# Cross-attention over 1500 keys: keys and values loaded in quarters of a chunk, one behind every slot, the mask's rows in thirds

## The chip, the core and the metric

The kernel runs on one core of one Trainium2 chip. The time is the device's, in microseconds, of one execution of the whole program: 32 batches, one launch. Durations inside it come from one profiled execution.

## What is computed

```python
# x (32, 56, 512), ctx (32, 1500, 512), all float32; 32 heads of 16
xn   = (x - mean(x)) * rsqrt(var(x) + 1e-5) * gamma + beta
Q    = split_heads(xn @ Wq.T)          # 32 heads
K, V = split_heads(ctx), split_heads(ctx)   # the context itself, no projection
s    = where(mask, einsum('bhsd,bhtd->bhst', Q, K) * 16**-0.5, -inf)
attn = einsum('bhst,bhtd->bhsd', softmax(s), V)
out  = x + attn.reshape(B, S, 512) @ Wout.T
```

The mask is of shape (32, 1500), one row per batch. Keys come in twice: once transposed by the host (`kt`, hidden dimension on the partitions), once as they are (`ctx`, used as values, keys on the partitions).

## The kernel before

**Tiling.** A batch has 1500 keys in 3 chunks of 500, and a chunk has 4 slots of 125 keys: 12 slots per batch, 384 in all. `kT` holds two batches of transposed keys, as [128 partitions, batch parity, chunk, 4 blocks of heads `g`, 4 slots `k`, 125 keys]: within a chunk the blocks come first, then the slots. `v_stage` has two stages of one chunk of values (125 partitions, 4 slots, 512 columns); GpSimd copies a chunk from there into `v` (L429), where each head's values stand beside ones, so that one matmul gives both the weighted sum and the denominator.

**A slot on TensorE** (its loop is the last block of the program): four score tiles for the maxima of a batch ahead (`score_tile`, L262, bf16, into two ring banks), four matmuls that spread the maxima (L295), 32 score matmuls (`score_blocks`, L303), 64 matmuls of the values of the slot before (`times_values`, L319), and in some slots a part of the output projection (L278). After the last of the values it raises `pv_done`, which so counts finished slots. The score tiles run a batch ahead: at the slots 10 and 11 of batch b they are those of batch b + 2, chunk 0; then chunk 0 goes on at slots 0 and 1 of batch b + 1, and so on.

**The other engines.** ScalarE makes the exponentials of a slot in two instructions (L385, L387), and at slot 0 it copies the sums of the batch before (L394). VectorE adds the mask's rows (`mask_tile`) to each score tile and takes its maximum in one instruction (L341), two instructions per tile with the readout; in slots 3 and 4 it also swaps (L370) and inverts (L377) the denominators of the batch before. GpSimd copies values (L429), spreads queries and maxima, and folds the sums (L438, L447, L450) and divides (L458).

**SyncE's queue** issues every DMA, in the order written out by hand at the end of its block. It waits for `pv_done` and then issues. In each batch b, at slot 0: the keys of batch b + 1, chunk 2 (1000 KB), the values of batch b, chunk 2 (1000 KB). At slot 4: keys of batch b + 2, chunk 0, values of batch b + 1, chunk 0, the mask's rows of batch b + 2 (112 partitions, 328 KB), and in even batches the store of a result and the load of a residual (224 KB each). At slot 8: keys of batch b + 2, chunk 1, values of batch b + 1, chunk 1. So 2 MB start in one go every four slots. `load_v` also waits for `v_ready`, GpSimd's copy out of the stage that is to be overwritten. Values of chunk c are copied by GpSimd (`spread_values`) in the order chunk 1 and 2 of batch b, then chunk 0 of batch b + 1; chunk 1's copy stands ahead of `fold_heads`, chunk 2's behind `divide_heads`.

The end of the program stores the last two results with the residual's load in between, when no keys or values move.

**Lines the prediction's steps touch:** L222 keys' load, L228 values' load, L231 mask's load, L237 residual's load, L241 result's store, and the lines above.

Of the kernel before, what the change touches and what calls it, by code (L numbers as in the profile page):

```python
# [18 lines left out]
BLOCKS, TILES_R, ROW = 4, 4, 32  # L19
# [69 lines left out]
def build(nc, x, kt, ctx, mask_lanes, mask_rows, wq_t, wout_t, gamma, beta, out):  # L89
    with ExitStack() as stack:  # L90
# [127 lines left out]
        out_rows = out.rearrange("(i b) s n -> i (b s) n", b=2)  # L218


        def load_k(sp, b, c):
            sp.dma_start(kT[:, b % 2, c].rearrange("p g k m -> p (g k m)"), kt[b, c]).then_inc(k_landed[b % 2][c], 16)  # L222

        def load_v(sp, b, c):
            n = CHUNKS * b + c
            src = ctx[b, KEYS * c:KEYS * (c + 1), :].rearrange("(m k) n -> m k n", k=CHUNK)
            wait_over(sp, v_ready, n - STAGES + 1)
            sp.dma_start(v_stage[0:LANES, n % STAGES], src).then_inc(v_landed[n % STAGES], 16)  # L228

        def load_mask(sp, b):  # L230
            sp.dma_start(mask_tile[0:PAIR_Q, b % 2, :], mask_add[b:b + 1].broadcast_to([PAIR_Q, CONTEXT])  # L231
                         ).then_inc(mask_tile_landed[b % 2], 16)

        def load_residual(sp, d):
# [15 lines left out]
        def score_tile(pe, unit):  # L250

            _, b, t = unit
            c, g, r = t // PAIRS, t % PAIRS // TILES_R, t % TILES_R
            if t == 0:
                pe.wait_ge(qdb_ready, b + 1)
            if t % PAIRS == 0:
                pe.wait_ge(k_landed[b % 2][c], 16 * (b // 2 + 1))
            bank = ring_bank(pe, unit)
            rows = slice(ROW * r, ROW * (r + 1))
            keys = kT[rows, b % 2, c, g].rearrange("p k m -> p (k m)").bitcast(BF16)  # L260
            keys = keys.rearrange("p (n h) -> p n h", h=2)[:, :, 1]
            nc.tensor.matmul(bank[0:PAIR_Q, 0:KEYS], qdb[rows, b % 2, g, :], keys,  # L262
                             start=True, stop=True).then_inc(ring_filled, 1)
# [19 lines left out]
        def begin_scores(pe, b, k):  # L283

            if k % CHUNK == 0:
                pe.wait_ge(k_landed[b % 2][k // CHUNK], 16 * (b // 2 + 1))
            if k == 0:
                pe.wait_ge(rows_spread, b + 1)
                pe.wait_ge(qd_ready, b + 1)
# [46 lines left out]
        def take_tile(dve, b, t, bank, sums):  # L336
            c, j = t // PAIRS, t % TILES_R * BLOCKS + t % PAIRS // TILES_R
            if t == 0:
                dve.wait_ge(mask_tile_landed[b % 2], 16 * (b // 2 + 1))
                wait_over(dve, neg_ready, b)  # L340
            nc.vector.tensor_tensor_reduce(  # L341
                out=sums, in0=bank[0:PAIR_Q, 0:KEYS],
# [79 lines left out]
        def spread_values(pool, b, c):  # L422

            n = CHUNKS * b + c
            pool.wait_ge(v_landed[n % STAGES], 16 * (n // STAGES + 1))
            wait_over(pool, pv_done, CHUNK * (n - CHUNKS + 1))
            halves = v[0:LANES, c].rearrange("p k i (h d) -> p (k i) h d", d=HEAD_DIM)[:, :, 0:3:2, :]
            staged = v_stage[0:LANES, n % STAGES].rearrange("p k (i h d) -> p (k i) h d", h=2, d=HEAD_DIM)
            nc.gpsimd.tensor_copy(halves, staged).then_inc(v_ready, 1)  # L429
# [34 lines left out]
        def _(sp):  # L464
# [9 lines left out]
            sp.dma_start(rows_u8[:, :], mask_rows).then_inc(mask_landed, 16)  # L474
            sp.dma_start(lanes_u8[0:LANES, :], mask_lanes).then_inc(mask_landed, 16)
            load_x(1)
            load_k(sp, 0, 0)
            for u in range(2, UNITS):
                load_x(u)
            load_k(sp, 0, 1)  # L480
            load_k(sp, 0, 2)
            sp.wait_ge(mask_added, 1)
            sp.dma_start(mask_add, rows_add[:, :]).then_inc(mask_stored, 16)
            load_k(sp, 1, 0)
            sp.wait_ge(mask_stored, 16)
            load_mask(sp, 0)
            load_mask(sp, 1)
            load_v(sp, 0, 0)
            sp.dma_start(woutT[:, :, :], wout_t.rearrange("(c p) n -> p c n", p=128)).then_inc(wout_landed, 16)
            load_k(sp, 1, 1)  # L490
            load_k(sp, 1, 2)
            sp.wait_ge(filled, FILLS)
            load_v(sp, 0, 1)
            load_v(sp, 0, 2)
            for b in range(BATCH):
                if b > 0:
                    if b < end:
                        sp.wait_ge(pv_done, SLOTS * b)
                        load_k(sp, b + 1, 2)
                    sp.wait_ge(pv_done, SLOTS * b)  # L500
                    load_v(sp, b, 2)
                if b < end:
                    sp.wait_ge(pv_done, SLOTS * b + CHUNK)
                    if b + 2 < BATCH:
                        load_k(sp, b + 2, 0)
                    load_v(sp, b + 1, 0)
                    if b + 2 < BATCH:
                        wait_taken(sp, ("tile", b, MAX_TILES - 1))
                        load_mask(sp, b + 2)
                if b % 2 == 0:  # L510
                    if b > 2:
                        store_result(sp, b // 2 - 2)
                    if b > 0:
                        load_residual(sp, b // 2 - 1)
                if b + 2 < BATCH:
                    sp.wait_ge(pv_done, SLOTS * b + 2 * CHUNK)
                    load_k(sp, b + 2, 1)
                if b < end:
                    sp.wait_ge(pv_done, SLOTS * b + 2 * CHUNK)
                    load_v(sp, b + 1, 1)  # L520
            store_result(sp, BATCH // 2 - 2)
            load_residual(sp, BATCH // 2 - 1)
            store_result(sp, BATCH // 2 - 1)
# [250 lines left out]
```

## Time and profile before

| | |
|---|---|
| median of 3 runs | 1591.01 us (1583.68 to 1594.36) |
| profiled execution, its own time | 1581.49 us |
| its span, first to last instruction | 1579.5 us |
| TensorE busy | 1390.2 us, 88% |
| VectorE busy | 1088.9 us, 69% |
| ScalarE busy | 769.3 us, 49% |
| GpSimd busy | 389.4 us, 25% |
| moved by DMA | 226.30 MB, mean 143 GB/s |
| DMA packets | 39249, of them 26882 of 2 to 8 KB |
| granted TensorE clock, mean | 0.934 |

The busy share of an engine says how full it is, not what it waits for; the views by wait, by queue and by stretch in the section below say that. The clock is the share of 2.4 GHz that was granted to TensorE.

### The profile page before, as it was taken

The page shows a single profiled execution, that of the slowest core. Times are in us where ns is not written, and L with a number is a line of the kernel's source. Part 1 is how long each engine was busy: PE and PEld are TensorE (multiplying, and loading weights), DVE is VectorE, ACT ScalarE, POOL GpSimd, SP SyncE. Part 2 cuts the span into 40 slices and gives each one's busy share as a digit, 9 for nine tenths or more (in the row PEclk, how much of TensorE's full clock was granted, in tenths as well). Part 3 has the DMA queues.
Part 4 walks back from the last instruction along what each step waited for, and adds up shares of the span by engine and source line. Part 5 has one row for each costly group of instructions (what it writes and reads, how often), then busy time and mean ns, then how long its engine had stood idle before and what let it go on. Part 6 is the DMA issues. An engine that isn't in the chain of part 4 may idle for free.

```text
span 1579.5 us, 88078 instructions
## 1 busy us (share of the span) xinstructions
PE 1390.2 (88%) x40736; PEld 1074.7 (68%) x40736; DVE 1088.9 (69%) x3452; ACT 769.3 (49%) x847; POOL 389.4 (25%) x371
## 2 busy tenths in 40 slices
PE   6999888899888988988888988989889888989986
PEld 4347767677676766766676776777677667767776
DVE  6557776777676767667777767777777676767741
ACT  2225454554554545454455545545454554544553
POOL 1012222332231133232133323222332231232221
PEclk8989998999999999899999999999999998998999
DMA  9214343443444444343434334344443443433420
GB/s 282 69 53 152 135 169 132 162 158 126 168 153 151 152 144 149 127 162 134 166 131 168 147 138 157 144 172 146 151 154 126 176 150 143 149 139 127 158 94 20
DMA packets 39249, 226.30 MB, mean 143 GB/s; under 512 B 4546, under 2 KB 4578, under 8 KB 26882
## 3 DMA queue, kind: packets, MB, share of 16 engines
q1 hardware_dynamic: 38882, 220.68, 38.4%
q8 instruction: 320, 5.24, 1.4%
q14 instruction: 47, 0.39, 0.1%
HBM read 216.90 MB, written 3.77 MB: 140 GB/s over the span
## 4 chain that ended last, share of the span: by engine, by line
PE 66%; DVE 23%; issue 9%; ACT 2%; DMA 0%; POOL 0%; SPq 0%; POOLq 0%; DVEq 0%; ACTq 0%
PE ps L319 21%; DVE masked L341 20%; PE ps L262 19%; PE ps L303 13%; PE ps L278 5%; PE ps L697 4%; PE ps L295 2%; DVE den_inv L377 2%; ACT probs L385 1%; PE ps L269 1%; DVE tile_max L341 1%; DMA v<-in_wq_t 0%; PE ps L688 0%; DVE den L370 0%; DVE probs L602 0%
## 5 line engine op out<-in xcount | busy, mean ns | idle before, releaser
L341 DVE CUSTOM_DVE_ANT_0 masked<-ps,mask_tile 112x500 bf16<-112x500 f32 x1536 | 974.2, 673 | 406.2 <-PE ps L262 391.0
L385 ACT ACTIVATE probs<-ps,mask_bias 125x1344 f32<-125x1344 f32 x384 | 530.3, 1381 | 711.9 <-PE ps L303 711.9
L262 PE MATMUL ps<-kT,qdb 32*112 32x500 bf16 x1536 | 498.3, 433 | 46.3 <-DVE tile_max L341 34.5
L303 PE MATMUL ps<-qd,kT 32*125 32x112 f32 x12288 | 498.6, 284 | 28.8 <-issue 28.6
L303 PEld LDWEIGHTS ps<-qd,kT 32*125 32x125 f32 x12288 | 494.9, 197 | 38.5 <-issue 34.1
L319 PE MATMUL ps<-probs,v 125*32 125x56 f32 x24576 | 429.3, 224 | 61.0 <-issue 59.1
L319 PEld LDWEIGHTS ps<-probs,v 125*32 125x32 f32 x24576 | 360.8, 117 | 159.9 <-issue 150.5
L262 PEld LDWEIGHTS ps<-kT,qdb 32*112 32x112 bf16 x1536 | 158.0, 128 | 203.4 <-DVE tile_max L341 150.0
L387 ACT ACTIVATE probs<-ps,mask_bias 125x448 f32<-125x448 f32 x384 | 240.4, 626 | 0.0
L295 PE MATMUL ps<-max_rows,ones_row 4*125 4x448 bf16 x1536 | 222.7, 400 | 11.6 <-issue 5.5
L429 POOL COPY v<-v_stage 125x2048 f32<-125x2048 f32 x96 | 181.5, 1891 | 75.5 <-DMA v_stage<-in_ctx 75.4
L418 POOL TENSOR_TENSOR max_rows<-rows,own_block 128x448 bf16<-128x448 f32 x32 | 29.8, 932 | 662.9 <-DVE rows L364 662.9
L341 DVE DVE_READ_ACCUMULATOR2_ANT tile_max<- 112x1 f32 x1536 | 126.6, 82 | 0.0
L458 POOL TENSOR_TENSOR attnT<-heads,den_inv 128x224 f32<-128x224 f32 x32 | 21.0, 656 | 366.9 <-DVE den_inv L377 366.9
L278 PE MATMUL ps<-woutT,attnT 128*112 128x128 f32 x512 | 76.3, 296 | 9.4 <-POOL attnT L458 5.1
L278 PEld LDWEIGHTS ps<-woutT,attnT 128*112 128x112 f32 x512 | 64.0, 189 | 25.5 <-DVE tile_max L341 12.9
L295 PEld LDWEIGHTS ps<-max_rows,ones_row 4*125 4x125 bf16 x1536 | 66.3, 135 | 18.6 <-issue 9.9
L697 PE MATMUL ps<-v 128*128 128x448 f32 (+2 forms) x160 | 66.9, 540 | 3.0 <-DMA v<-in_wq_t 2.2
L377 DVE RECIPROCAL den_inv<-den 128x56 f32<-128x56 f32 x128 | 62.9, 495 | 0.2
L358 DVE TENSOR_TENSOR result<-ps,x_res 112x128 f32<-112x128 f32 x64 | 18.6, 290 | 44.7 <-PE ps L278 41.5
L438 POOL TENSOR_TENSOR picked_den<-raw,own_head 128x448 f32<-128x448 f32 x32 | 29.8, 932 | 62.1 <-ACT raw L394 62.0
L662 ACT COPY qT<-ps 128x448 f32<-128x448 f32 (+2 forms) x20 | 9.1, 456 | 66.1 <-PE ps L697 65.9
(48 smaller groups left out, 293.5 us busy)
## 6 DMA issues: line engine op xcount, KB each, us to landing
kT<-in_kt SPq DMA_DIRECT2D x96, 1000.0 KB, 5.3
v_stage<-in_ctx SPq DMA_DIRECT2D x96, 1000.0 KB
mask_tile<-mask_add SPq DMA_DIRECT2D x32, 328.1 KB, 13.6
x_res<-in_x SPq DMA_DIRECT2D x16, 224.0 KB, 13.7
out<-result SPq DMA_DIRECT2D x16, 224.0 KB, 13.7
probs<-in_x SPq DMA_DIRECT2D x14, 224.0 KB, 9.8
v<-in_wq_t SPq DMA_DIRECT2D x1, 1024.0 KB, 6.7
woutT<-in_wout_t SPq DMA_DIRECT2D x1, 1024.0 KB, 20.3
```

The lines of the kernel that those rows point to most:

```text
L262: nc.tensor.matmul(bank[0:PAIR_Q, 0:KEYS], qdb[rows, b % 2, g, :], keys, start=True, stop=True).then_inc(ring_filled, 1)
L278: mm = nc.tensor.matmul(bank[0:PAIR_Q, 0:OUT_COLS], attnT[:, d % 2, g, :], woutT[:, g, OUT_COLS * part:OUT_COLS * (part + 1)], start=(g == ...
L295: nc.tensor.matmul(ps[0:LANES, score_bank(n, r), 0:BANK_Q], ones_row[rows, :], max_rows[rows, b % 2].rearrange("p g n -> p (g n)"), start= ...
L303: mm = nc.tensor.matmul(ps[0:LANES, score_bank(SLOTS * b + k, r), PAIR_Q * g:PAIR_Q * (g + 1)], kT[rows, b % 2, k // CHUNK, g, k % CHUNK, ...
L319: mm = nc.tensor.matmul(acc[ROW * r:ROW * (r + 1), i, :], v[0:LANES, c, k % CHUNK, TILES_R * g + r, HEAD_DIM * e:HEAD_DIM * e + ROW], prob ...
L341: nc.vector.tensor_tensor_reduce(out=sums, in0=bank[0:PAIR_Q, 0:KEYS], in1=mask_tile[0:PAIR_Q, b % 2, KEYS * c:KEYS * (c + 1)], scale=1.0, ...
L377: nc.vector.reciprocal(den_inv[:, g], den[:, g]).then_inc(den_inverted, 1)
L385: nc.scalar.activation(probs[0:LANES, k % PROBS, 0:HELD_ROWS], ps[0:LANES, 0:HELD_ROWS, 0:BANK_Q], ACT.Exp, bias=bias, scale=SCALE).then_i ...
L387: nc.scalar.activation(probs[0:LANES, k % PROBS, HELD_ROWS], ps[0:LANES, score_bank(n, HELD_ROWS), 0:BANK_Q], ACT.Exp, bias=bias, scale=SC ...
L418: nc.gpsimd.tensor_tensor(max_rows[:, b % 2], rows[:].unsqueeze(1).broadcast_to([128, BLOCKS, PAIR_Q]), own_block[:].unsqueeze(2).broadcas ...
L429: nc.gpsimd.tensor_copy(halves, staged).then_inc(v_ready, 1)
L697: mm = nc.tensor.matmul(bank, wqT[:, h, 128 * c:128 * (c + 1)], xT[u % 2][:, h, 0:w], start=(h == 0), stop=(h == BLOCKS - 1))
```

## The change

Every load of a chunk of keys or values becomes four loads of a quarter. A quarter of keys is one block `g` of heads (128 partitions, rows of 2000 bytes in place of 8000); a quarter of values is one slot `k` of the chunk (125 partitions, rows of 2048 bytes in place of 8192). A batch's mask rows come in three thirds, one per chunk (112 partitions, rows of 1000 bytes). The waits count all four or three pieces, so a consumer starts once the whole chunk, or the whole mask of a batch, has landed. In the loop SyncE waits for `pv_done` once per slot and issues one quarter of keys and one of values there; a third of the mask's rows goes behind slots 1, 4 and 7. Which chunk is loaded during which four slots is as before, so the first quarter starts where the whole chunk did, and the last one three slots later. The store and the residual stay at slot 4. The loads ahead of the loop keep their places, as runs of four or three.

```diff
-        def load_k(sp, b, c):
-            sp.dma_start(kT[:, b % 2, c].rearrange("p g k m -> p (g k m)"), kt[b, c]).then_inc(k_landed[b % 2][c], 16)
-
-        def load_v(sp, b, c):
+        def load_k(sp, b, c, g):
+            sp.dma_start(kT[:, b % 2, c, g].rearrange("p k m -> p (k m)"), kt[b, c, :, KEYS * g:KEYS * (g + 1)]
+                         ).then_inc(k_landed[b % 2][c], 16)
+
+        def wait_keys(pe, b, c):
+            pe.wait_ge(k_landed[b % 2][c], 16 * BLOCKS * (b // 2 + 1))
+
+        def load_v(sp, b, c, k):
             n = CHUNKS * b + c
             src = ctx[b, KEYS * c:KEYS * (c + 1), :].rearrange("(m k) n -> m k n", k=CHUNK)
-            wait_over(sp, v_ready, n - STAGES + 1)
-            sp.dma_start(v_stage[0:LANES, n % STAGES], src).then_inc(v_landed[n % STAGES], 16)
-
-        def load_mask(sp, b):
-            sp.dma_start(mask_tile[0:PAIR_Q, b % 2, :], mask_add[b:b + 1].broadcast_to([PAIR_Q, CONTEXT])
+            if k == 0:
+                wait_over(sp, v_ready, n - STAGES + 1)
+            sp.dma_start(v_stage[0:LANES, n % STAGES, k], src[:, k]).then_inc(v_landed[n % STAGES], 16)
+
+        def load_mask(sp, b, c):
+            keys = slice(KEYS * c, KEYS * (c + 1))
+            sp.dma_start(mask_tile[0:PAIR_Q, b % 2, keys], mask_add[b:b + 1, keys].broadcast_to([PAIR_Q, KEYS])
                          ).then_inc(mask_tile_landed[b % 2], 16)
...
             for b in range(BATCH):
-                if b > 0:
-                    if b < end:
-                        sp.wait_ge(pv_done, SLOTS * b)
-                        load_k(sp, b + 1, 2)
-                    sp.wait_ge(pv_done, SLOTS * b)
-                    load_v(sp, b, 2)
...
+                for k in range(SLOTS):
+                    step = k % CHUNK
+                    wait_over(sp, pv_done, SLOTS * b + k)
+                    if (b, k) >= (0, CHUNK):
+                        of, c = (b + 2, k // CHUNK - 1) if k >= CHUNK else (b + 1, CHUNKS - 1)
+                        if of < BATCH:
+                            load_k(sp, of, c, step)
+                        of, c = (b + 1, k // CHUNK - 1) if k >= CHUNK else (b, CHUNKS - 1)
+                        if of < BATCH:
+                            load_v(sp, of, c, step)
+                    if k in (1, 4, 7) and b + 2 < BATCH:
+                        if k == 1:
+                            wait_taken(sp, ("tile", b, MAX_TILES - 1))
+                        load_mask(sp, b + 2, k // 3)
+                    if k == CHUNK and b % 2 == 0 and b > 0:
+                        if b > 2:
+                            store_result(sp, b // 2 - 2)
                         load_residual(sp, b // 2 - 1)
```

## Rows read from the trace of the kernel before

**Rows 1.** The page and the cores: chain that ended last; span and mean clock.
```profile
PE 66%; DVE 23%; issue 9%; ACT 2%; DMA 0%; POOL 0%; SPq 0%; POOLq 0%; DVEq 0%; ACTq 0%
...
core 0: 1579.5 us, clock 0.934
```
**Rows 2.** Waits, whole span: who waited for what, us in total, times, longest.
```profile
PE ps L319 <- issue: 59.1, 46, 3.3
...
PE ps L303 <- issue: 28.6, 28, 3.0
```
**Rows 3.** Timeline of TensorE: start us, us, engine line op, shapes, count, idle before.
```profile
862.58 0.88 PE L319 MATMUL ps<-probs,v 125*32 125x56 f32 x51
866.07 0.39 PE L319 MATMUL ps<-probs,v 125*32 125x56 f32 x13 [2.62 <-issue]
```
**Rows 4.** Timeline of SyncE's queue, same columns, 856 to 858 us.
```profile
856.88 0.35 SPq L222 DMA_DIRECT2D kT<-in_kt  x1
857.27 0.33 SPq L228 DMA_DIRECT2D v_stage<-in_ctx  x1
857.65 0.31 SPq L231 DMA_DIRECT2D mask_tile<-mask_add  x1
```
**Rows 5.** DMA queues, 123.2 to 1486.2 us: kind: packets, MB, share of 16 engines.
```profile
q8 instruction: 296, 4.85, 1.5%
```
**Rows 6.** DMA queues, 857.3 to 863.2 us: the only two that moved anything.
```profile
q1 hardware_dynamic: 338, 1.62, 85.2%
q14 instruction: 1, 0.01, 0.4%
```
**Rows 7.** DMA queues, 863.2 to 866.1 us: the queue q8.
```profile
q8 instruction: 1, 0.02, 2.6%
```
**Rows 8.** Stretches: length, busy PE, PEld, DVE, ACT, POOL; clock, DMA share, GB/s.
```profile
859.00:861.00 2.00, 1.85 (x79) 1.54 (x83) 1.41 (x7) 1.77 (x2) 2.00 (x2) 1.00 0.97 362
864.00:869.00 5.00, 2.85 (x65) 1.94 (x69) 2.08 (x7) 0.98 (x1) 0.00 (x0) 0.88 0.34 136
867.78:874.61 6.83, 6.75 (x168) 5.40 (x169) 4.30 (x14) 3.24 (x4) 0.00 (x0) 0.50 0.19 76
874.60:912.10 37.50, 33.18 (x1074) 25.81 (x1066) 28.00 (x92) 20.11 (x23) 12.00 (x11) 1.00 0.44 160
1003.00:1048.00 45.00, 40.39 (x1309) 32.00 (x1309) 33.87 (x109) 23.35 (x25) 12.00 (x11) 1.00 0.44 160
1571.50:1572.00 0.50, 0.50 (x4) 0.50 (x4) 0.00 (x0) 0.00 (x0) 0.00 (x0) 0.50 0.99 283
```
**Rows 9.** Timeline of SyncE's queue: first and last load of keys in the loop.
```profile
123.20 0.35 SPq L222 DMA_DIRECT2D kT<-in_kt  x1
...
1486.24 0.35 SPq L222 DMA_DIRECT2D kT<-in_kt  x1
```
**Rows 10.** Timeline of ScalarE: slot 0 of two batches that follow each other.
```profile
980.22 1.38 ACT L385 ACTIVATE probs<-ps,mask_bias 125x1344 f32<-125x1344 f32 x1 [1.75 <-PE ps L303]
...
1022.89 1.38 ACT L385 ACTIVATE probs<-ps,mask_bias 125x1344 f32<-125x1344 f32 x1 [1.72 <-PE ps L303]
```
**Rows 11.** Timeline of TensorE, 980 to 1023 us: the instructions behind "issue".
```profile
1003.02 0.29 PE L319 MATMUL ps<-probs,v 125*32 125x56 f32 x4 [1.11 <-issue]
...
1020.75 0.59 PE L319 MATMUL ps<-probs,v 125*32 125x56 f32 x27 [0.27 <-issue]
```
**Rows 12.** The page, DMA issues: xcount, KB each, us from issue to landing.
```profile
kT<-in_kt SPq DMA_DIRECT2D x96, 1000.0 KB, 5.3
```
**Rows 13.** DMA queues, 1540 to 1563 us, the only one that moved anything.
```profile
q8 instruction: 7, 0.11, 2.2%
```
**Rows 14.** Timeline of GpSimd, 1021 to 1026 us.
```profile
1021.81 1.89 POOL L429 COPY v<-v_stage 125x2048 f32<-125x2048 f32 x1 [0.97 <-DMA v_stage<-in_ctx]
...
1025.37 0.93 POOL L438 TENSOR_TENSOR picked_den<-raw,own_head 128x448 f32<-128x448 f32 x1 [1.67 <-ACT raw L394]
```
**Rows 15.** Timeline of VectorE, 990 to 991 us.
```profile
990.42 0.41 DVE L370 STREAM_SHUFFLE den<-den_across 128x224 f32<-128x224 f32 x1
```

More of the change, by code:

```diff
@@ L256, in score_tile @@
             if t % PAIRS == 0:
-                pe.wait_ge(k_landed[b % 2][c], 16 * (b // 2 + 1))
+                wait_keys(pe, b, c)
             bank = ring_bank(pe, unit)
@@ L285, in begin_scores @@
             if k % CHUNK == 0:
-                pe.wait_ge(k_landed[b % 2][k // CHUNK], 16 * (b // 2 + 1))
+                wait_keys(pe, b, k // CHUNK)
             if k == 0:
@@ L338, in take_tile @@
             if t == 0:
-                dve.wait_ge(mask_tile_landed[b % 2], 16 * (b // 2 + 1))
+                dve.wait_ge(mask_tile_landed[b % 2], 16 * CHUNKS * (b // 2 + 1))
                 wait_over(dve, neg_ready, b)
@@ L424, in spread_values @@
             n = CHUNKS * b + c
-            pool.wait_ge(v_landed[n % STAGES], 16 * (n // STAGES + 1))
+            pool.wait_ge(v_landed[n % STAGES], 16 * CHUNK * (n // STAGES + 1))
             wait_over(pool, pv_done, CHUNK * (n - CHUNKS + 1))
@@ L476, in _ @@
             load_x(1)
-            load_k(sp, 0, 0)
+            for g in range(BLOCKS):
+                load_k(sp, 0, 0, g)
             for u in range(2, UNITS):
                 load_x(u)
-            load_k(sp, 0, 1)
-            load_k(sp, 0, 2)
+            for g in range(BLOCKS):
+                load_k(sp, 0, 1, g)
+            for g in range(BLOCKS):
+                load_k(sp, 0, 2, g)
             sp.wait_ge(mask_added, 1)
             sp.dma_start(mask_add, rows_add[:, :]).then_inc(mask_stored, 16)
-            load_k(sp, 1, 0)
+            for g in range(BLOCKS):
+                load_k(sp, 1, 0, g)
@@ L485, in _ @@
             sp.wait_ge(mask_stored, 16)
-            load_mask(sp, 0)
-            load_mask(sp, 1)
-            load_v(sp, 0, 0)
+            for c in range(CHUNKS):
+                load_mask(sp, 0, c)
+            for c in range(CHUNKS):
+                load_mask(sp, 1, c)
+            for k in range(CHUNK):
+                load_v(sp, 0, 0, k)
             sp.dma_start(woutT[:, :, :], wout_t.rearrange("(c p) n -> p c n", p=128)).then_inc(wout_landed, 16)
-            load_k(sp, 1, 1)
-            load_k(sp, 1, 2)
+            for g in range(BLOCKS):
+                load_k(sp, 1, 1, g)
@@ L492, in _ @@
+            for g in range(BLOCKS):
+                load_k(sp, 1, 2, g)
             sp.wait_ge(filled, FILLS)
-            load_v(sp, 0, 1)
-            load_v(sp, 0, 2)
+            for k in range(CHUNK):
+                load_v(sp, 0, 1, k)
+            for k in range(CHUNK):
+                load_v(sp, 0, 2, k)
             for b in range(BATCH):
-                if b > 0:
-                    if b < end:
-                        sp.wait_ge(pv_done, SLOTS * b)
-                        load_k(sp, b + 1, 2)
-                    sp.wait_ge(pv_done, SLOTS * b)
-                    load_v(sp, b, 2)
[L502 to L513, printed above, removed]
-                        load_residual(sp, b // 2 - 1)
[L515 to L520, printed above, removed]
```

## The prediction

> **What bounds the kernel now.** I read the page first, for the chain that ended last: it lies on TensorE for 66% of the span, on VectorE for 23%, and for 9% on "issue", which is time in which an engine waited for nothing that the profile shows; the granted clock averages 0.934 [rows 1]. The list of waits gives the matmuls of the values and of the scores 59.1 and 28.6 us behind "issue", in 46 and 28 stalls [rows 2]: few and long, 1.2 us each. No semaphore, bank or operand explains them, so I went to the timeline of one. TensorE stops inside the values of a slot, between the 51st and 52nd of 64 equal matmuls, for 2.62 us up to 866.07 [rows 3].
>
> The next view is the queue of SyncE. At 856.9 to 857.7 it began the keys, the values and the mask's rows of one step, 1000, 1000 and 328 KB [rows 4]. Then the DMA queues by packet. Queue q8, of kind "instruction", is the stream of TensorE's own instructions: between 123.2 and 1486.2 us it moved 296 packets of 16 KB [rows 5]. In the 5.9 us after the loads began it moved none [rows 6]. The next packet came in the 2.9 us after that [rows 7], and TensorE ran on at 866.07, inside the same stretch. So TensorE had used up its instructions and the next ones stood behind data. The table by stretch shows what they stood behind: from 859 to 861 us the DMA engines were busy to 97% [rows 8].
>
> The stall has a second price. Right behind it, from 867.78 to 874.61, the granted clock is 0.50 (1.2 GHz), where it was 1.00 (2.4 GHz) before [rows 8]. There TensorE issued 168 matmuls in 6.83 us, 24.6 per us; in the 37.5 us at full clock that follow it issued 1074, 28.6 per us [rows 8]. A stretch at half clock thus does 14% less. The mean clock of 0.934 [rows 1] means (1 - 0.934) x 2 x 1579.5 = 208 us at half clock, some 29 us of loss.
>
> **What the stalls cost in all.** First by batch, as that counts what the stalls drag along too. SyncE's first and last load of keys in the loop are at 123.20 and 1486.24 us [rows 9]; 90 of them make 89 steps of four slots, 356 slots of 12 to the batch, so a batch takes 1363.04 / 29.67 = 45.94 us. The batch whose first exponentials start at 980.22, the next batch's at 1022.89 [rows 10], took 42.67 us, with only two stalls in it, of 1.11 and 0.27 us [rows 11], and without a fall of the clock. Without them it is 42.67 - 1.11 - 0.27 = 41.29 us. The difference, 4.65 us, times 31.9 batches (383 slots from first to last) is 148 us. Second by parts: 59.1 + 28.6 of stalls [rows 2] and 29 of clock are 117 us, less than 148, since the slots behind a stall (scores, exponentials, VectorE's tiles) start late too. I take 148, as that stretch is the kernel itself at work with its bursts but nearly without stalls.
>
> **The change, part by part.** *Bytes* stay the same. *Keys*: one load of 1000 KB on four slots becomes four of 250 KB, one a slot. In before the load lands 5.3 us after its issue [rows 12]. A transfer of about the size of a quarter is seen at the end, where a result's store and a residual's load of 224 KB each follow each other: a half microsecond of that has the DMA engines at 99% [rows 8], at 283 GB/s; 448 KB at that rate are 1.6 us, 0.8 us for one and 0.9 us for a quarter. I take 1.0 us in which a fetch can be kept waiting, against 5.9 us behind keys and mask in the case above.
>
> *Values*: a quarter still goes in rows over 125 partitions. From 864 to 869 us, with the keys landed and values still moving, the DMA engines are busy to 34%, at 136 GB/s [rows 8]: the values use a third of them. Bounds: nothing, or 250 KB at 136 GB/s, 1.9 us a slot, if the fetch used those engines. I take nothing, since q8 delivered in that state [rows 7], as it did not while all were busy.
>
> *Mask*: 328 KB in one step become three of 109 KB in three slots, 0.4 us each at 283 GB/s, so that 1.0 us of keys is followed by 0.4 us of mask in three slots of twelve.
>
> *What is left of the stalls.* In 1540 to 1563 us, without data, q8 moved 7 packets in 23 us [rows 13], so instructions can come every 3.8 us or faster. A batch needs 296 / 29.67 = 10.0 packets, one in 4.1 us at 41.3 us a batch. The cover is 0.3 us. A slot of 3.4 us holds 1.0 us of keys, so a fetch meets them 29 times in 100 and is late by 0 to 1.0 us; what passes the cover is 0.29 x 0.7 x 0.7 / 2 = 0.07 us a fetch, 23 us over 319 fetches. The other bound is 0, since VectorE's tiles (23% of the chain [rows 1]) are the next limit in many slots and take in small holes. I take 6 us. Stalls so short should leave the clock alone: neither of the two in [rows 11] was followed by a fall, the clock being 1.00 from 1003 to 1048 us [rows 8].
>
> *Issues*: three more for keys, three more for values in every four slots, at 0.28 to 0.35 us [rows 4]: SyncE issues at most three in a slot, about 1.1 of 3.4 us, and nothing waits for it. At the start some 25 more issues of 0.4 us, 10 us together, are spread over the time in which TensorE works on its projections from inputs that have landed; that is their cover, and without it they would cost up to 10 us. I take 0.
>
> *Lateness*: the last quarter of each chunk is issued three slots later. The tightest is the second chunk of values. GpSimd copied it at 1021.81, and began the denominators at 1025.37 [rows 14]. Its last quarter would be issued one slot before the load at slot 0, about 1021.8. On a third of the engines 250 KB take about what 1000 KB of keys take on all, 5.3 us to landing: 1027.1, the copy ends at 1029.0, 3.6 us late, and the three steps up to their sum, at most 0.93 us each [rows 14], end at 1031.8. VectorE takes the denominators 10.2 us into a batch (990.42 [rows 15] less 980.22 [rows 10]), here at 1033.1. So it is hidden by 1.3 us; without that cover each us late costs up to 31 us over the kernel. Keys and mask of slot 7 are used at slot 10, two slots later.
>
> Sum: 1579.5 - 148 + 6 = 1437.5 us of span, plus 2.0 around it (1581.49 - 1579.5) gives 1439.5; stalls drag along some 26% more than themselves (148 to 117), so that the 1.38 us taken off the good batch should be 1.74, 0.36 x 31.9 = 11 us more, which gives 1428. I predict **1435 us**, between the two. The profiled execution lies 9.5 us under the median of the three runs, 1591.01, and within their range.
>
> **What the Trainium skill says.** Its page "Runtime: NRT & Kernel Launch", section "Instruction fetch mechanics", says that instructions come in blocks of 16 KiB, 256 instructions, with the next page fetched while the current one is executed; the trace agrees on the size (296 packets, 4.85 MB [rows 5]). It adds that the fetch is hidden behind the issuing of instructions; by that rule nothing is to be gained and the time would stay 1581.5. The stall in [rows 3, 6, 7] disagrees. Its page "DMA: Bandwidth & Descriptors", section "Queues, rings and completion order", says that each DMA engine takes turns between queues, and drains a whole packet of some 9 to 17 descriptors before it switches. By that, pieces of a quarter of the bytes make a turn shorter, which is this change's direction; that a fetch would get in between keys and mask is not what [rows 6] shows.
>
> **The rivals.** *Partial* (0.20): fetches still come late, each a little, because the cover is only 0.3 us and every slot now has a burst. If half of the 148 us stays, the time is 1581.5 - 74 = 1507. For it: 12 bursts a batch instead of 3. Against: each is a quarter as long.
> *No change* (0.06): the stall isn't set by the length of the bursts, or another wait takes its place, such as GpSimd's late values. Time 1575 to 1597.
> *Slower* (0.07): one mechanism, at the fetch. Bursts of keys come once a slot, and fetches once in 1.2 slots (10.0 to a batch); if nearly every fetch has to wait out a whole burst of 1.0 us, each loses 0.7 us past the cover, 319 x 0.7 = 223 us against 148 now, so 1581.5 + 75 = 1656 us. It decides from 0.46 us lost per fetch (148 / 319). Against: 29 in 100 is what chance gives.
> *Faster than forecast* (0.05): every slot as the quickest, no stall, under 1400 us.
> *The forecast* (0.62): 1400 to 1470.
>
> **How the numbers follow.** A measurement of this kernel can tell about 1% from no change. Forecast, faster case and the partial one lie all below -1%: 0.87. Within 1%: 0.06. Slower: 0.07. The range takes the forecast and most of the partial case, 1400 to 1525, some 0.8 in all.
>
> **What would show it.** Stalls behind "issue" on TensorE down from some 90 us to under 25; mean clock at 0.98 or above; q8 with a packet in every 5 us; batches of 40.5 to 42 us; loads of keys every 3.4 us. The forecast is wrong if q8 still pauses for 4 us or more, if the clock stays near 0.93, or if VectorE waits for the denominators.

## The result and the profile after

| | before | after |
|---|---|---|
| median | 1591.76 us (4 runs) | 1496.97 us (4 runs, 1490.18 to 1505.58) |
| ratio | 1 | 0.9415, 95% interval 0.9356 to 0.9475 |
| profiled execution, span | 1579.5 us | 1495.6 us |
| mean granted clock | 0.934 | 0.963 |
| stalls of the matmuls behind "issue", all lines | 98.0 us in 83 | 52.5 us in 73 |
| q1 (data), share of 16 engines' span | 38.4% | 47.7% |

The change is 5.9% faster, 95 us of the 156 that were forecast. The stalls and the clock both moved the forecast way and both stopped half-way. The rows below answer to [rows 1, 2, 12]. First the page of after: the chain by engine, and the keys' issues with count, size and landing.

```profile
PE 66%; DVE 26%; issue 6%; ACT 2%; DMA 0%; POOL 0%; SPq 0%; POOLq 0%; DVEq 0%; ACTq 0%
...
kT<-in_kt SPq DMA_DIRECT2D x384, 250.0 KB, 3.1
```

The waits of after, whole span:

```profile
PE ps L325 <- issue: 36.1, 44, 2.7
...
PE ps L309 <- issue: 13.4, 24, 2.3
```

"issue" went from 9 to 6% of the chain; the two waits fell from 87.7 to 49.5 us. A quarter of keys lands 3.1 us after its issue, a whole chunk took 5.3 [rows 12]: a quarter of the bytes needs 58% of the time.

The queue of SyncE, first and last load of keys in the loop, answers to [rows 9].

```profile
119.94 0.35 SPq L222 DMA_DIRECT2D kT<-in_kt  x1
...
1415.67 0.35 SPq L222 DMA_DIRECT2D kT<-in_kt  x1
```

Between them lie 359 slots: 1295.73 / 359 x 12 = 43.31 us a batch, where before took 45.94 and the forecast said 40.5 to 42.

Whose instructions q8 carries can be checked on all stalls. In before 72 of the 73 stalls of 0.3 us or more in the slots end 1.2 to 1.6 us after a packet of q8 has ended, in after 52 of 53 end 1.2 to 1.7 us after one. And from one such stall of before to the next TensorE starts 254 matmuls and weight loads, or a multiple of 254 to within 13, in 71 of 72 cases; 81,472 of them over the 320 packets of the whole run are 255 to a packet. So each stall stands at the end of a packet's worth of instructions and ends with the next packet.

Where the rest is. Sorted by slot (a slot counted from the start of its exponentials), the timeline of before gives 56 of its 98 us of stalls to slot 6, which comes behind the load of keys, values and mask at slot 4; the rest is spread. In after slot 6 still has 24 us, 22.7 of them in 14 stalls of even batches and only 1.7 in odd ones. Even batches are those that also store a result and load a residual at slot 4. One of them is batch 18. The timeline of SyncE's queue in after:

```profile
888.21 0.35 SPq L222 DMA_DIRECT2D kT<-in_kt  x1
888.60 0.33 SPq L233 DMA_DIRECT2D v_stage<-in_ctx  x1
888.97 0.50 SPq L237 DMA_DIRECT2D mask_tile<-mask_add  x1
889.52 0.42 SPq L247 DMA_DIRECT2D out<-result  x1
889.99 0.43 SPq L243 DMA_DIRECT2D x_res<-in_x  x1
```

The timeline of TensorE in after, the matmul behind the stall:

```profile
897.39 0.41 PE L325 MATMUL ps<-probs,v 125*32 125x56 f32 x7 [2.57 <-issue]
```

The stretches of after, columns as in [rows 8]:

```profile
890.50:892.50 2.00, 2.00 (x85) 1.69 (x89) 1.41 (x5) 1.59 (x2) 1.95 (x2) 1.00 0.85 86
892.50:894.50 2.00, 1.82 (x77) 1.29 (x76) 2.00 (x7) 1.12 (x1) 0.00 (x0) 1.00 0.93 209
897.40:904.00 6.60, 6.60 (x147) 5.79 (x150) 3.70 (x11) 1.91 (x2) 0.00 (x0) 0.52 0.37 113
```

The DMA queues of after from 889.9 to 895.3 us: packets, MB, share of 16 engines.

```profile
q1 hardware_dynamic: 627, 1.03, 93.0%
q8 instruction: 1, 0.02, 1.1%
```

Five loads and stores start within 1.8 us, and the DMA engines are busy to 85 and 93% for four microseconds, in the first two at only 86 GB/s. One packet of instructions began in these 5.4 us, at their end (894.82, 5.7 us after the one before it had ended), TensorE stood for 2.57 us, and the clock halved behind it. It is the picture of [rows 3 to 8] with less behind it.

Two ordinary slots of after, without mask or residual: the stretches that hold a quarter of keys (first and third) and those that do not.

```profile
701.50:703.00 1.50, 1.37 (x45) 0.79 (x43) 1.50 (x7) 0.80 (x1) 0.00 (x0) 1.00 0.75 209
703.00:704.90 1.90, 1.89 (x88) 1.65 (x80) 1.07 (x3) 1.58 (x3) 0.00 (x0) 1.00 0.35 125
704.90:706.50 1.60, 1.42 (x52) 0.89 (x52) 1.60 (x7) 0.94 (x1) 0.42 (x1) 1.00 0.67 190
706.50:708.00 1.50, 1.50 (x65) 1.21 (x57) 0.91 (x3) 0.97 (x2) 1.50 (x2) 1.00 0.34 131
```

The keys' burst takes 1.5 us, not the 1.0 of the forecast, and the values keep a third of the engines busy all the time between.

### The profile page after: what moved, and what is told of

Its sections match the earlier page's. It is cut to its first block, busy times and chain, and to the rows that moved or that the text cites. A ratio compares the mean times of both kernels' runs of the same rounds, so it can differ in the third digit from the quotient of the medians.

```text
span 1495.6 us, 88664 instructions
## 1 busy us (share of the span) xinstructions
PE 1352.0 (90%) x40736; PEld 1037.6 (69%) x40736; DVE 1088.4 (73%) x3452; ACT 769.7 (51%) x847; POOL 388.8 (26%) x371
## 3 DMA queue, kind: packets, MB, share of 16 engines
q1 hardware_dynamic: 125986, 220.71, 47.7%
## 4 chain that ended last, share of the span: by engine, by line
PE 66%; DVE 26%; issue 6%; ACT 2%; DMA 0%; POOL 0%; SPq 0%; POOLq 0%; DVEq 0%; ACTq 0%
DVE masked L347 22%; PE ps L325 22%; PE ps L268 21%; PE ps L309 12%; PE ps L284 5%; PE ps L707 4%; PE ps L301 2%; DVE den_inv L383 2%; ACT probs L391 1%; PE ps L275 1%; DVE tile_max L347 1%; DMA v<-in_wq_t 0%; DVE probs L612 0%; PE ps L698 0%; DVE den L376 0%
## 5 line engine op out<-in xcount | busy, mean ns | idle before, releaser
L309 PE MATMUL ps<-qd,kT 32*125 32x112 f32 x12288 | 478.7, 277 | 13.6 <-issue 13.4
L309 PEld LDWEIGHTS ps<-qd,kT 32*125 32x125 f32 x12288 | 475.1, 190 | 21.7 <-issue 18.0
L325 PE MATMUL ps<-probs,v 125*32 125x56 f32 x24576 | 410.4, 218 | 38.0 <-issue 36.1
L325 PEld LDWEIGHTS ps<-probs,v 125*32 125x32 f32 x24576 | 343.7, 113 | 132.7 <-issue 125.5
L301 PE MATMUL ps<-max_rows,ones_row 4*125 4x448 bf16 x1536 | 213.7, 391 | 7.9 <-ACT probs L391 5.5
L383 DVE RECIPROCAL den_inv<-den 128x56 f32<-128x56 f32 x128 | 63.1, 496 | 0.2
L707 PEld LDWEIGHTS ps<-v 128*128 128x128 f32 x160 | 27.5, 216 | 18.2 <-issue 12.5
```

Source lines behind the costliest of these rows:

```text
L301: nc.tensor.matmul(ps[0:LANES, score_bank(n, r), 0:BANK_Q], ones_row[rows, :], max_rows[rows, b % 2].rearrange("p g n -> p (g n)"), start= ...
L309: mm = nc.tensor.matmul(ps[0:LANES, score_bank(SLOTS * b + k, r), PAIR_Q * g:PAIR_Q * (g + 1)], kT[rows, b % 2, k // CHUNK, g, k % CHUNK, ...
L325: mm = nc.tensor.matmul(acc[ROW * r:ROW * (r + 1), i, :], v[0:LANES, c, k % CHUNK, TILES_R * g + r, HEAD_DIM * e:HEAD_DIM * e + ROW], prob ...
L383: nc.vector.reciprocal(den_inv[:, g], den[:, g]).then_inc(den_inverted, 1)
L707: mm = nc.tensor.matmul(bank, wqT[:, h, 128 * c:128 * (c + 1)], xT[u % 2][:, h, 0:w], start=(h == 0), stop=(h == BLOCKS - 1))
```

## The experiments

Two theories stood at the start. **A**: the packets of TensorE's instructions wait behind data on the DMA engine that carries them; keys, mask and residual pass over that engine, the values (over 5 engines) do not. **B**: any data in flight holds them. Each kernel was timed against the kernel before; ratios are to that.

| kernel | median us | ratio, 95% interval | stalls, matmuls, us (x) | clock |
|---|---|---|---|---|
| after | 1497.0 | 0.9415, 0.9356 to 0.9475 | 52.5 (73) | 0.963 |
| keys_only | 1562.0 | 0.9853, 0.9798 to 0.9908 | 87.0 (88) | 0.936 |
| values_only | 1575.9 | 0.9895, 0.9858 to 0.9932 | 92.9 (75) | 0.940 |
| mask_whole | 1509.5 | 0.9508, 0.9462 to 0.9554 | 63.1 (61) | 0.954 |
| halves | 1571.3 | 0.9904, 0.9872 to 0.9936 | 98.0 (107) | 0.955 |
| store_apart | 1477.4 | 0.9288, 0.9218 to 0.9357 | 44.2 (72) | 0.974 |
| eighths | 1517.2 | 0.9578, 0.9507 to 0.9650 | 59.2 (89) | 0.967 |
| before_eleven | 1656.6 | 1.0416, 1.0349 to 1.0482 | 133.2 (81) | 0.908 |
| one_row | 1424.9 | 0.8984, 0.8954 to 0.9014 | 10.9 (21) | 0.989 |
| values_real | 1437.7 | 0.9083, 0.9032 to 0.9134 | 18.4 (39) | 0.986 |

The stalls are the waits of TensorE's matmuls behind "issue" over the whole span of the profiled execution, all lines together. before_eleven is an edit of the kernel before, the others of after. one_row and values_real leave most of the input out, the others compute all of it.

### One part of the change alone

Keys in quarters, values and mask as before; and values in quarters, keys and mask as before. The edit to the changed kernel for the first (values and mask whole again):

```diff
-            sp.dma_start(v_stage[0:LANES, n % STAGES, k], src[:, k]).then_inc(v_landed[n % STAGES], 16)
+            if k % 4 == 0:
+                sp.dma_start(v_stage[0:LANES, n % STAGES, k:k + 4], src[:, k:k + 4]).then_inc(v_landed[n % STAGES], 16)
...
-                    if k in (1, 4, 7) and b + 2 < BATCH:
+                    if k == CHUNK and b + 2 < BATCH:
```

> Keys in quarters, one a slot; values whole (1000 KB) at slots 0, 4 and 8, mask whole at slot 4, so one part of the change alone. Theory A (TensorE's instruction packets wait behind data on the DMA engine that carries them, and only the keys, the mask and the residual use that engine): most of the gain is here, 1500 to 1530 us, with long stalls left only at the mask's step. Theory B (any data in flight slows the fetch, through memory or through the number of bytes in flight): values of 1000 KB in one go still stall it, about half the gain, 1540 to 1570 us.

And for the second (keys and mask whole again):

```diff
-            sp.dma_start(kT[:, b % 2, c, g].rearrange("p k m -> p (k m)"), kt[b, c, :, KEYS * g:KEYS * (g + 1)]
-                         ).then_inc(k_landed[b % 2][c], 16)
+            if g % 4 == 0:
+                sp.dma_start(kT[:, b % 2, c, g:g + 4].rearrange("p g k m -> p (g k m)"),
+                             kt[b, c, :, KEYS * g:KEYS * (g + 4)]).then_inc(k_landed[b % 2][c], 16)
```

> Values in quarters, one a slot; keys whole at slots 0, 4 and 8, mask whole at slot 4. Theory A: no gain, 1580 to 1600 us, stalls behind issue stay near 98 us and the clock near 0.93. Theory B: about half the gain, 1540 to 1570 us.

Measured: 1562.0 and 1575.9 us. For keys_only A asked for 1500 to 1530 us and is missed; 1562 lies in the range of B, but is a quarter of the change's gain and not half. values_only lies 4 us below A's range and far from B's; its stalls (92.9 us) and clock (0.940) are near those that A gave. Alone they give 1.5 and 1.1%, together, with the mask still whole (mask_whole, below), 4.9%. The parts need each other. The page of keys_only shows one reason, the landing of a quarter of keys, which took 3.1 us in after:

```profile
kT<-in_kt SPq DMA_DIRECT2D x384, 250.0 KB, 4.7
```

The packets of q8 show the rest. A chunk's loads begin at the slots 0, 4 and 8, 87 such steps in batches 1 to 29. Counted is how many packets start 2 to 4 us after TensorE has finished the slot before, when the load's data move. The matmuls and their order are the same in all these kernels, so one_row (below), with one row in each load, says what the program alone would give.

| kernel | keys | values | packets that start 2 to 4 us on |
|---|---|---|---|
| one_row | one row | one row | 39 |
| values_real | one row | quarters | 39 |
| after | quarters | quarters | 31 |
| halves | halves | halves | 21 |
| keys_only | quarters | whole | 19 |
| values_only | whole | quarters | 5 |
| before | whole | whole | 4 |

Whole keys keep the packets out, quarters of values keep none out, and whole values beside quarters of keys keep out more than quarters of both. So A holds where it says that keys hold the packets and that a load of values by itself doesn't. What it lacks is that whole values make the keys land later and hold longer. That they do so on the DMA engines that both use is argued from the landing times, not shown.

### One part of the change undone: the mask

```diff
-                    if k in (1, 4, 7) and b + 2 < BATCH:
-                        if k == 1:
-                            wait_taken(sp, ("tile", b, MAX_TILES - 1))
-                        load_mask(sp, b + 2, k // 3)
+                    if k == CHUNK and b + 2 < BATCH:
+                        wait_taken(sp, ("tile", b, MAX_TILES - 1))
+                        load_mask(sp, b + 2, 0)
```

> The changed kernel with the mask's rows whole again at slot 4 (328 KB): one part undone. Theory A: the stall in slot 6 grows by up to 0.8 us in every batch and is followed by half clock in odd batches too; 20 to 40 us more than the changed kernel, 1515 to 1535 us. Rival, that the thirds are worth nothing since each meets a page too: 1490 to 1505 us.

Measured: 1509.5 us, 12.5 more than after, under the 20 to 40 expected and above the rival's 1505, with intervals that overlap a little (0.9508 from 0.9462, 0.9415 to 0.9475). The direction is that of a burst at slot 4 that is longer; the size was overrated.

### Other sizes of a load

Halves: 500 KB of keys and of values behind every second slot. The edit to the changed kernel:

```diff
+            if g % 2 == 0:
+                sp.dma_start(kT[:, b % 2, c, g:g + 2].rearrange("p g k m -> p (g k m)"),
+                             kt[b, c, :, KEYS * g:KEYS * (g + 2)]).then_inc(k_landed[b % 2][c], 16)
...
+            if k % 2 == 0:
+                sp.dma_start(v_stage[0:LANES, n % STAGES, k:k + 2], src[:, k:k + 2]).then_inc(v_landed[n % STAGES], 16)
```

> The changed kernel with keys and values in halves of a chunk (500 KB), one of each behind every second slot; the mask's thirds, store and residual as there. A burst of keys lasts twice as long as a quarter, and there are half as many. Theory A with a cover of about 0.3 us: what counts is how far a fetch is kept waiting past its cover, and that grows faster than the burst; between the quarters and whole chunks, 1510 to 1540 us. Rival, that each burst costs the same whatever its length: half the loss of the quarters, 1455 to 1480 us.

Eighths: each quarter of keys in two loads, half a slot apart, with store and residual apart as in the next section.

```diff
+                        if of_k < BATCH:
+                            load_k(sp, of_k, c_k, step, (0,))
...
+                        if of_k < BATCH:
+                            sp.wait_ge(scored, SLOTS * b + k + 2)
+                            load_k(sp, of_k, c_k, step, (1,))
```

> The changed kernel with store and residual at slots 5 and 6, and each quarter of keys cut in two by slots of the chunk: one eighth (128 rows of 1000 bytes) ahead of the quarter of values, the other half a slot later, once the next slot's scores are made. To be compared with the kernel that only has store and residual apart, 1477 us. Theory A, bursts scale with the bytes: 1445 to 1465 us, clock 0.98 or more. Rival, a burst has a fixed part (first packets take several times as long as the later ones), so that halving the bytes leaves most of its length and doubles their number: 1475 to 1500 us.

Measured: halves 1571.3 us, 1.0% under before and worse than even A said: twice as many bursts as whole chunks, each landed 3.9 us behind its issue (5.3 whole), and as much stalled time in all (98.0 us against 98.0). Eighths 1517.2 us, against 1477.4 with quarters (store_apart): 40 us worse, beyond what its rival said. So neither longer nor shorter was better here. Why is not separated: both kernels also begin loads at other places of the program, eighths half-way through each slot. Shorter rows cost more engine time for the same bytes: 38.4% of 1579.5 us in before is 607, 47.7% of 1495.6 in after 713, 51.4% of 1515.8 in eighths 779. (Of before's 39249 packets 22304 are of 2 to 8 KB; the 26882 of its table are all those under 8 KB.) The data queue in the page of after (packets, MB, share):

```profile
q1 hardware_dynamic: 125986, 220.71, 47.7%
```

and in the page of eighths:

```profile
q1 hardware_dynamic: 181282, 220.73, 51.4%
```

### The step with five transfers

```diff
-                    if k == CHUNK and b % 2 == 0 and b > 0:
-                        if b > 2:
-                            store_result(sp, b // 2 - 2)
+                    if k == CHUNK + 1 and b % 2 == 0 and b > 2:
+                        store_result(sp, b // 2 - 2)
+                    if k == CHUNK + 2 and b % 2 == 0 and b > 0:
                         load_residual(sp, b // 2 - 1)
```

> The changed kernel with the result's store at slot 5 and the residual's load at slot 6 of even batches, in place of both at slot 4. In the changed kernel 11 of the stalls behind issue, 1.2 to 2.7 us each and some 21 us together, lie in slot 6 of even batches and are each followed by half clock. Theory A: they shrink below 1 us, the clock rises from 0.963 to 0.975 or more, and the time falls by 15 to 35 us to 1460 to 1482 us. Rival (the page boundary in slot 6 is late for another reason, such as the mask's third): no change, 1490 to 1505 us.

Measured: 1477.4 us, ratio 0.9288 (0.9218 to 0.9357): as expected, 20 us under after, though the intervals touch. Slot 6 of even batches went from 22.7 us of stalls in 14 to 3.2 in 6; the clock rose from 0.963 to 0.974. The other slots did not gain: 39.5 us in 63 stalls, where after had 28.1 in 56. The store and the residual may meet packets in their new slots; that is not shown. The waits of store_apart, whole span, are

```profile
PE ps L325 <- issue: 26.3, 46, 1.8
PE ps L309 <- issue: 15.1, 21, 1.9
```

and no stall above 1.9 us. It is the fastest kernel with the full computation here.

### What the traffic costs in all

The changed kernel with every load issued and waited for, but one partition's row in each from the third batch on; and the same with the values in full.

```diff
+            rows = 128 if b < 2 else 1
-            sp.dma_start(kT[:, b % 2, c, g].rearrange("p k m -> p (k m)"), kt[b, c, :, KEYS * g:KEYS * (g + 1)]
+            sp.dma_start(kT[0:rows, b % 2, c, g].rearrange("p k m -> p (k m)"), kt[b, c, 0:rows, KEYS * g:KEYS * (g + 1)]
```

> The changed kernel with the same loads issued and waited for, but from the third batch on each load of keys, values and mask brings one partition's row only (the rest of the tiles keeps older data, so most of the input is left out). It prices all that the traffic costs. Theory A: no stall behind issue but for those at the store and the residual of even batches, clock 0.98 or more, batches of 40.3 to 40.8 us, 1400 to 1430 us. Rival, that TensorE's instructions come late whatever the traffic: above 1450 us.

The second differs from the first in one line:

```diff
-            rows = LANES if n < 3 else 1
+            rows = LANES
```

> The changed kernel with all its loads issued, values in full quarters, but keys and mask of one row each from the third batch on (that part of the input is left out); residual and store in full. Against the run with one row of everything, 1425 us, it prices the values' quarters alone, which go over 5 engines. Theory A, as the prediction had it (values leave the instruction packets alone): 1420 to 1430 us. Theory C (the values' rows hold them too, which would explain that quarters of one kind alone gave 1.5% and 1.1% and both together 5%): 1440 to 1470 us.

Measured: 1424.9 and 1437.7 us. Without the traffic TensorE's instructions come in time: 10.9 us of stalls. The span and clock of one_row:

```profile
core 0: 1424.3 us, clock 0.989
```

The waits of one_row, whole span:

```profile
PE ps L328 <- issue: 7.5, 16, 1.4
PE ps L312 <- issue: 1.9, 2, 1.3
```

So data in flight costs the kernel before 1591.8 - 1424.9 = 167 us (160 by 1585.2, the median of its runs beside one_row) and the changed one 72 us. Of these 72 the values' quarters are 13 (between what A and C said, intervals 0.8954 to 0.9014 against 0.9032 to 0.9134), and keys, mask and the way they add up the other 59. Of the 72, 42 are stalls (52.5 - 10.9), and by the prediction's 14% some 11 are half clock; the remaining 19 are an estimate by difference. How the values' 13 us arise is open, as their quarters kept no packet out in the count above.

### Which DMA engine?

Four kernels loaded keys over fewer engines, as a load's partitions divide, to see which engine carries the instructions. How many engines a load uses can be read from its packets: in the third kernel the key packets in flight at once, in the middle of an undisturbed load, were 5, 6, 7, 9, 10, 11, 13, 14, 15 and 16 for 125, 102, 119, 81, 100, 110, 117, 126, 120 and 128 rows. The first is the kernel before with keys, mask, residual and store each in two parts, of 110 partitions and of the rest; the keys' part of the edit:

```diff
+            for p in (slice(0, 110), slice(110, 128)):
+                sp.dma_start(kT[p, b % 2, c].rearrange("p g k m -> p (g k m)"), kt[b, c, p]
+                             ).then_inc(k_landed[b % 2][c], 16)
```

> The kernel before, whole chunks in one go, but each load of keys cut by partitions into 110 and 18, and each load or store of mask, residual and result into 110 and 2: the same bytes at the same times, over fewer than 16 DMA engines (if the split follows the divisors of the partition count, 11 and 9 engines). Theory A with the instruction packets on an engine that these leave free: the stalls vanish without any quartering, clock 0.98 or more, 1400 to 1440 us. Theory A with the packets on one of the engines still used: no gain or a loss (bursts last 16/11 as long), 1580 to 1640 us. Theory B: no change, 1580 to 1600 us.

Measured: 1656.6 us, 4.2% slower than before and beyond the 1640 of its worst case, stalls 133.2 us. The 110 rows of the keys use 11 engines, each longer, and the packets are not free of them: 6 of the 87 steps counted above have one, where before has 4. It has the same bytes as before at the same slots, in bursts that are longer, but also in twice as many transfers.

The second gives each of a batch's three chunks of keys its own division:

```diff
+KEY_ROWS = [(102, 25, 1), (81, 27, 18, 2), (119, 7, 2)]
...
+            at = 0
+            for rows in KEY_ROWS[c]:
+                sp.dma_start(kT[at:at + rows, b % 2, c].rearrange("p g k m -> p (g k m)"), kt[b, c, at:at + rows]
+                             ).then_inc(k_landed[b % 2][c], 16)
+                at += rows
```

> The kernel before, with keys whole but cut by partitions so that each chunk's load uses another number of DMA engines: chunk 2 (slot 0) 119 + 7 + 2 rows, 7 engines; chunk 0 (slot 4) 102 + 25 + 1, 6 engines; chunk 1 (slot 8) 81 + 27 + 18 + 2, 9 engines. The keys on 11 engines still held the instruction packets back, the values on 5 do not. If an engine's place in the row is fixed and a load takes the first ones, the steps at which instruction packets start inside the keys' burst tell between which numbers the instruction packets' engine lies: free at all three: it is the tenth or eleventh; held at slot 8 alone: the eighth or ninth; held at slots 0 and 8: the seventh; held at all three: the sixth. If it is no fixed engine but the number of bytes in flight, the packets come late at all three alike.

Measured: 1680 us, one execution. The starts of q8's packets in the steps did not sort by 6, 7 and 9 engines; stalls were 98.0 us, as in before. The keys' packets of a chunk moved for 9.2 us in the median (3.6 in before) and the clock was 0.895; what of the loss is due to which was not separated. Inconclusive.

The third takes one_row and gives the keys back, whole chunks of as many rows as the list says, three batches (nine loads) for each entry:

```diff
+        KEY_ROWS = [125, 102, 119, 81, 100, 110, 117, 126, 120, 128]
...
+            if g % KEY_BLOCKS == 0:
+                rows = 128 if b < 2 else KEY_ROWS[(b - 2) // 3]
+                sp.dma_start(kT[0:rows, b % 2, c].rearrange("p g k m -> p (g k m)"), kt[b, c, 0:rows]
```

> From the third batch on only keys are loaded in bulk, whole chunks at slots 0, 4 and 8, and values and mask bring one row, so most of the input is left out. The number of partitions in the keys' load changes every three batches: 125, 102, 119, 81, 100, 110, 117, 126, 120, 128, which by their divisors are 5, 6, 7, 9, 10, 11, 13, 14, 15 and 16 DMA engines. Theory A with one fixed engine for TensorE's instructions: no stalls behind issue up to some number between 5 and 11, and from there on stalls of several us at nearly every load (bursts last 5 to 8 us on few engines). Rival, that the instruction packets go round the engines: stalls grow steadily with the number of engines. Rival, that it is the bytes in flight and no engine: stalls in all ten groups alike.

Measured: 1534.4 us, one execution. Stalled time per group of nine loads, in the order 125, 102, 119, 81, 100, 110, 117, 126, 120, 128 rows: 2.3, 4.1, 11.3, 3.0, 5.3, 9.4, 4.0, 5.7, 18.1, 4.4 us. The waits of TensorE in engines, first group (5 engines):

```profile
PE ps L332 <- issue: 1.9, 4, 0.9
PE ps L316 <- issue: 0.5, 1, 0.5
```

The same in its ninth group (15 engines):

```profile
PE ps L316 <- issue: 12.8, 5, 4.0
PE ps L275 <- issue: 3.7, 1, 3.7
PE ps L332 <- issue: 1.5, 4, 0.6
```

Five engines hold little, fifteen much, but there is no clean step and no steady growth. Nine loads are too few: where in a burst a packet falls depends on the program.

The fourth differs from the third in having two entries only, one for the even and one for the odd batches:

```diff
-                rows = 128 if b < 2 else KEY_ROWS[(b - 2) // 3]
+                rows = 128 if b < 2 else (102, 119)[b % 2]
```

> As the run with ten groups (only keys in bulk, whole chunks; most of the input left out), but with two sizes in turn: 102 partitions (6 engines) in even batches, 119 (7 engines) in odd ones. Both bring 17 rows of 8000 bytes to each engine used, bursts of the same length at the same places. Theory A with the instruction packets on the seventh engine alone: stalls of over 2 us only behind loads of 119 rows, and at least three times the stalled time there. With them on the sixth engine or below, or going round: both alike.

Measured: 1495.6 us, one execution; behind 45 loads of 102 rows 14.3 us in 21 stalls, one above 1.5 us; behind 45 of 119 rows 33.8 us in 27, seven above 1.5 us. A factor of 2.4 where A asked for 3, and one stall of 2.2 us where it allowed none. It leans to the seventh engine. Counted as above, of the 44 steps with 119 rows 4 have a packet 2 to 4 us on, where one_row has 22 at the same steps; but of the 43 with 102 rows 10 have one, against 17, so six engines seem to keep some out too, which the seventh alone can't explain. **Which engines carry the instructions stays open.**

## Why the prediction was right, and where it was not

- **What bounds the kernel: right.** Stalls behind "issue" are TensorE waiting for its instruction packets, held by data, with the clock as a second price. one_row shows it by taking the data away and leaving the work, the issues and the waits: stalls from 52.5 to 10.9 us, clock 0.989. The 72 of 73 stalls that end 1.2 to 1.6 us behind a packet of q8 show that it is this queue, and the count of packets (39 of 87 steps without keys, 4 with whole keys) that data hold it.
- **What the stalls cost, 148 us: nearly right.** Before less one_row is 160 to 167 us. The one good batch that the estimate rested on had 1.38 us of stalls in it and slots behind them that were late too; the 11 us added for that were in the right direction.
- **A quarter of keys, 1.0 us: too small.** Its burst is 1.5 us at 67 to 75% of the engines. The rate was taken from a half microsecond inside two transfers side by side (283 GB/s [rows 8]), where the start of one is covered by the other. Engine time for the same bytes grew from 607 to 713 us.
- **Values, nothing: the reason right, the size wrong.** Quarters of values alone keep no packet out (39 of 87 steps, as with none), as the reading of [rows 7] had it, yet values_real gives 13 us. And the values' size matters through the keys, which landed after 4.7 us beside whole values and after 3.1 beside quarters.
- **What is left of the stalls, 6 us: the step that failed.** It measured 72 us (1497.0 - 1424.9), with an upper bound of 23 in the working. Three things were wrong in it: 1.0 for 1.5 us; values at nothing; and chance as the rule for how packets meet bursts. A batch has 10.0 packets (296 / 29.67), nearly a whole number, so a packet's place in the program moves little from batch to batch: slot 6 was hit in 30 of 32 batches in before. If it falls behind the fullest step, it does so again and again. The step with store and residual had been left where it was and costed at nothing; store_apart prices it at about 20 us. Of the other 46 us (72 - 6 - 20) values_real gives the values 13; how the rest splits is not shown. The cover of 0.3 us was not too high: in one_row packets start as little as 3.3 us apart, under the 3.8 that were taken.
- **The clock stays up after short stalls: right for most.** But 11 stalls of slot 6 in even batches were 1.2 to 2.7 us, and 10 of them had a stretch of half clock of 3.4 or 6.8 us that began within them or up to 2 us behind. Seven more such stretches stood behind stalls of 0.6 to 1.1 us, where the prediction expected none. Mean clock 0.963, not 0.98.
- **Mask: direction right.** mask_whole costs 12.5 us more.
- **Lateness of the last values, hidden: right.** Batch 15 of after, whose slot 0 starts at 747.32, answers to [rows 14, 15]. The timeline of GpSimd:

```profile
751.50 1.89 POOL L435 COPY v<-v_stage 125x2048 f32<-125x2048 f32 x1 [5.71 <-DMA v_stage<-in_ctx]
...
755.14 0.66 POOL L453 TENSOR_TENSOR den_across<-picked_den 128x224 f32<-128x224 f32 x1
  ```

  The timeline of VectorE:

  ```profile
757.73 0.41 DVE L376 STREAM_SHUFFLE den<-den_across 128x224 f32<-128x224 f32 x1
```

  The sum of the denominators is there at 755.80, 1.9 us before it is taken; 1.3 had been worked out. In the whole run VectorE waits for it twice, 21.8 us, both behind 1438 us at the end, and before does so as well (twice, 20.5 us).
- **Issues and start, nothing: right.** The loop's first load of keys is at 119.94, earlier than before's 123.20.
- **Which case came.** The time is that of the rival called partial: 52.5 of 98.0 us of stalls are left, "each a little, because the cover is only 0.3 us and every slot now has a burst". It was given 1507 us and 0.20; the forecast's own 1400 to 1470 missed. Of the signs that it named for being wrong one came: q8 still paused for 5.7 us before the stall at 897.39. The batches of 43.31 us and the clock of 0.963 lie outside what it asked for as well. That the range of 1400 to 1525 holds 1497 is owed to the partial case, not to the sum.
- **The two rules of the Trainium skill.** That the fetch is hidden ("Runtime: NRT & Kernel Launch", "Instruction fetch mechanics") holds in one_row, at 11 us of stalls, and not beside loads. That an engine changes queues only after a packet of several descriptors ("DMA: Bandwidth & Descriptors", "Queues, rings and completion order") agrees in its direction: beside quarters 31 of 87 steps had a packet, beside whole loads 4. No run here shows the turns themselves.

## What to carry to other kernels

Where TensorE stalls for 1 to 3 us behind "issue" in the middle of equal matmuls, look at the queue of kind "instruction" and at what data transfers began in the 8 us before; then price it with a copy of the kernel whose loads bring one row. Cut such transfers to what the instruction stream can bear, all of them, since parts alone gave 1.5 and 1.1% and together 5%. Try more than one size: here 250 KB was better than 500 and than 125, and the reason is open. And don't let several start in the same step: moving one store and one load by a slot or two was worth about 20 us, an eighth of what the traffic cost.

## What was not expected of the hardware

- Cutting loads by four made them 18% dearer in engine time (607 to 713 us for 220.7 MB), rows of 2000 bytes in place of 8000; cutting the keys once more brought 779 us.
- Halves left the stalls where they were (98.0 us) and gave 1.0%, though each load landed in 3.9 us in place of 5.3, and quarters of keys and values together nearly halved the stalls.
- With a mask, a store and a load behind the keys the DMA engines were busy to 85% while they moved only 86 GB/s (890.5 to 892.5 us).
- Keys over 16 DMA engines kept instruction packets out almost wholly (4 of 87 steps, 39 without keys), quarters of values over 5 engines not at all (39).
